# Two attentions with 32-wide heads: the three score products of a head become one product of depth 96 on copies made by DMA

## What is computed

```python
Q = split_heads(Xn @ Wq + bq)
K = split_heads(Xn @ Wk + bk)
V = split_heads(Xn @ Wv + bv)
scores = jnp.einsum('bhqd,bhkd->bhqk', Q, K) / jnp.sqrt(jnp.float32(D_HEAD))
causal = jnp.tril(jnp.ones((n_ctx, n_ctx), dtype=bool))
scores = jnp.where(causal, scores, jnp.float32(-jnp.inf))
A = jax.nn.softmax(scores, axis=-1)
AV = jnp.einsum('bhqk,bhkd->bhqd', A, V)
AV = AV.swapaxes(-2, -3).reshape(X.shape[:-1] + (D_MODEL,))
return AV @ Wo + bo
```

## Time and profile before

| | us |
|---|---|
| median of 3 runs | 3378.17 (3377.19 to 3378.65) |
| span of the profiled execution | 3376.4 |
| a0, from its first weight load to the next stage's loads | 8.2 to 383.1 |
| a1, likewise | 785.6 to about 1235 |
| PE busy in the whole span | 2992.2 (89%) |

### The profile page before, as it was taken

One profiled execution on the slowest core, in us unless ns is written; L12 is line 12 of the kernel. 1 busy time (PEld: TensorE's weight loads), 2 busy tenths in 40 slices (PEclk: granted clock), 3 DMA queues, 4 the chain that ended last, 5 costly groups with the idle time before them and its releaser, 6 DMA issues. The chain is left out here.

```text
span 3376.4 us, 46857 instructions
## 1 busy us (share of the span) xinstructions
PE 2992.2 (89%) x16388; PEld 2260.9 (67%) x16388; DVE 1996.1 (59%) x5348; ACT 1551.2 (46%) x3598; POOL 1019.2 (30%) x1143
## 2 busy tenths in 40 slices
PE   6999799997999977978788767998689999989999
PEld 4777678885666645446566646775467777768887
DVE  5666587775555554233747767664678777742121
ACT  5777566664666652133222244444455555531000
POOL 3655333222444530000156640000133233322222
PEclk9999899998999987988899988999799999999999
DMA  2000301101000021203100020003100000020000
GB/s 87 2 2 1 113 32 32 32 32 63 1 2 1 2 67 64 100 7 117 66 4 4 2 101 1 1 1 119 34 1 1 1 1 1 1 103 13 13 13 13
DMA packets 65872, 105.51 MB, mean 31 GB/s; under 512 B 9315, under 2 KB 29795, under 8 KB 65509
## 3 DMA queue, kind: packets, MB, share of 16 engines
q1 hardware_dynamic: 65222, 102.41, 8.7%
q0 software_dynamic: 416, 0.10, 0.0%
HBM read 89.75 MB, written 12.85 MB: 30 GB/s over the span
## 5 line engine op out<-in xcount | busy, mean ns | idle before, releaser
L714 POOL TENSOR_SCALAR a_P<-a_P,a_rec 128x512 f32<-128x512 f32 (+3 forms) x256 | 301.5, 1190 | 350.9 <-DVE a_rec L872 350.9
L402 ACT ACTIVATE tree_value<-tree_bit,table_lut,tree_step 128x256 f32<-128x256 uint8 x496 | 275.3, 595 | 140.8 <-DVE tree_value L416 73.0
L416 DVE COPY_PREDICATED tree_value<-tree_bit,tree_value 128x256 f32<-128x256 uint8 x434 | 235.0, 547 | 133.3 <-ACT tree_value L402 104.9
L787 ACT ACTIVATE a_P<-a_P,a_low 128x384 f32<-128x384 f32 (+3 forms) x512 | 281.7, 558 | 25.0 <-DVE a_low L866 24.9
L101 PE MATMUL bank<-f_xT_hi,f_w_hi 128*128 128x512 f32 (+1 forms) x704 | 276.6, 393 | 14.0 <-DVE f_w_lo L1214 14.0
L102 PE MATMUL bank<-f_xT_hi,f_w_lo 128*128 128x512 f32 (+1 forms) x704 | 276.1, 392 | 0.0
L103 PE MATMUL bank<-f_xT_lo,f_w_hi 128*128 128x512 f32 (+1 forms) x704 | 275.7, 392 | 0.0
L1136 POOL CAST f_h_hi<-f_sg 128x512 fp32r<-128x512 f32 (+1 forms) x88 | 84.5, 961 | 587.6 <-DVE f_sg L1236 297.8
L866 DVE CUSTOM_DVE_ANT_0 a_P<-bank,a_causal 128x384 f32<-128x384 f32 (+3 forms) x512 | 222.9, 482 | 63.1 <-PE bank L949 62.6
L794 ACT ACTIVATE a_PT<-bank 128x512 f32<-128x512 f32 x320 | 174.2, 594 | 83.3 <-PE bank L960 82.6
L1236 DVE TENSOR_TENSOR f_sg<-bank,f_sg 128x512 f32<-128x512 f32 (+1 forms) x44 | 30.4, 691 | 269.4 <-PE bank L103 269.4
(11 more groups left out here) (464 smaller groups left out, 7922.7 us busy)
## 6 DMA issues: line engine op xcount, KB each, us to landing
f_w_raw<-in_f_w SPq DMA_DIRECT2D x11, 768.0 KB, 12.8
f_w_raw<-table_w SPq DMA_DIRECT2D x11, 768.0 KB, 11.2
tree_idx<-in_f_idx SPq DMA_DIRECT2D x62, 128.0 KB, 2.1
table_w<-tree_value SPq DMA_DIRECT2D x62, 128.0 KB, 1.7
x_res<-in_x SPq DMA_DIRECT2D x4, 1024.0 KB, 10.8
m_piece<-in_m_wq SPq DMA_DIRECT2D x2, 2048.0 KB, 12.1
m_piece<-in_m_wo SPq DMA_DIRECT2D x2, 2048.0 KB, 8.5
m_piece<-in_m_w_gate SPq DMA_DIRECT2D x2, 2048.0 KB, 10.4
```

The source lines that it names most:

```text
L402: act.activation(prog.tree_value[(h + to) % 4][:, :], prog.tree_bit[h % 2][0][:, :], ACT.Identity, bias=prog.table_lut[:, 2 * k:2 * k + 1] ...
L416: dve.copy_predicated(prog.tree_value[(h + keep) % 4][:, :], prog.tree_bit[h % 2][bit][:, :], prog.tree_value[(h + other) % 4][:, :]).then ...
L714: last = pool.tensor_scalar(Pr[j][:, g, col:col + n], Pr[j][:, g, col:col + n], rec[:, j, i, g:g + 1], None, ALU.mult)
L787: last = act.activation(Pr[j][:, k, col:col + n], Pr[j][:, k, col:col + n], ACT.Exp, bias=low[:, j, i, k:k + 1], scale=-1.0, accum_out=tot ...
```

## The change

Queries and keys are no longer used where ACT and DVE write them. `Q` and `K` shrink to one chunk, a landing place. From there SP copies, SBUF to SBUF, each head's 32 partitions three times into partitions 0 to 95 of a stacked tile: `QS` as hi, lo, hi (two turns), `KS` as hi, hi, lo (two turns in a0, one in a1). That is 12 DMAs of 64 KB for each Q and 12 for each K, where a1 has 16 of either and a0 16 and 4. One matmul 96 deep for each head and part of a chunk then gives the sum of the three products.

New waits: SP waits for the low part, and before writing a turn again for the last scores that read it (for K two waits, one for each pair of heads); ACT waits, before it writes Q or K, until the copies of the one before have landed; PE waits for the copies of Q once and for those of K at each pair of a unit's first chunk. In `ORDER`, VT and Q(0, 1) of a0 and two V of a1 stand ahead of the first scores instead of among them; in a0 T and K of the next row come earlier; DVE's statistics and POOL's roots of a0 follow.

```diff
-    Q, _ = prog.pair(name + "_Q", [P, DC, T])
-    turns = 2 if KC == 1 else 1
-    K = [prog.pair(f"{name}_K{i}", [P, KC, T])[0] for i in range(turns)]
+    Q, _ = prog.pair(name + "_Q", [P, T])
+    K, _ = prog.pair(name + "_K", [P, T])
+    K_TURNS = 2 if KC == 1 else 1
+    QS = [prog.sb(f"{name}_QS{i}", [P, G, T], F32R) for i in range(2)]
+    KS = [prog.sb(f"{name}_KS{i}", [P, G, T], F32R) for i in range(K_TURNS)]
+    DEPTH = 3 * HD
+    Q_COPIES, K_COPIES = (0, 1, 0), (0, 0, 1)
...
-                     [[[("Q", b, 3)], []], [[("Y", b - 1, 2)], [("T", n, 0)]], [[("Y", b - 1, 3)], [("T", n, 1)]]],
-                     [[[("T", n, 2)], [("T", n, 3)]], [[("Q", n, 0)], []], [[("K", n, 0)], []]],
+                     [[[("Q", b, 3)], [("T", n, 0)]], [[("Y", b - 1, 2)], [("T", n, 1)]], [[("Y", b - 1, 3)], [("T", n, 2)]]],
+                     [[[("T", n, 3)], [("K", n, 0)]], [[("Q", n, 0)], []], [[], []]],
...
-        beside = [[(("VT", 0, 0), 6)], [(("V", 0, 0), 7)], [(("Q", 0, 1), 4)]]
+        ORDER += [(("VT", 0, 0), 6), (("Q", 0, 1), 7)]
+        beside = [[(("V", 0, 0), 4)], [], []]
...
+                if kind == "Q":
+                    m = unit(at, k)
+                    sp.wait_ge(*read((kind, at, k)))
+                    if m >= 2:
+                        sp.wait_ge(*full(("S", 3 * (m - 2) + 2, G - 1)))
+                    for g in range(G):
+                        for i, half in enumerate(Q_COPIES):
+                            sp.dma_start(QS[m % 2][HD * i:HD * (i + 1), g, :].bitcast(F32), Q[half][HD * g:HD * (g + 1), :].bitcast(F32)).then_inc(q_in[m % 2].sem, 16)
...
+                        if i_ >= K_TURNS:
+                            sp.wait_ge(*full(("S", k_last_chunk(i_ - K_TURNS), some[1])))
...
+                    if kind == "Q" and unit(at, k):
+                        act.wait_ge(*q_stacked(unit(at, k) - 1))
...
+                    if j == 0:
+                        if k == 0:
+                            pe.wait_ge(*q_stacked(m))
+                        pe.wait_ge(*k_stacked(i_, k))
+                    for g in (2 * k, 2 * k + 1):
                         pe.wait_ge(*vacant(("S", at, g)))
...
+                        for i, (col, qt) in enumerate(PARTS[j]):
+                            n = (qt + 1) * P
+                            last = pe.matmul(ps[J.bank(("S", at, g))][:, col:col + n], QS[m % 2][0:DEPTH, g, qt * P:(qt + 1) * P],
+                                             KS[i_ % K_TURNS][0:DEPTH, g, 0:n], start=i == 0, stop=True, skip_group_check=True)
+                        last.then_inc(J.fills(("S", at, g)), 1)
```

More of the change, by code:

```diff
@@ L649, in attention32, with unit, q_stacked, k_number @@
     NQK = DC + KC
-    def unit(at):
-        return at[0] * DC + at[1]
+    q_in = [prog.count(f"q_in{i}") for i in range(2)]
+    k_in = [[prog.count(f"k_in{i}_{k}") for k in (0, 1)] for i in range(K_TURNS)]
+    Q_BYTES, K_BYTES = 16 * len(Q_COPIES) * G, 16 * len(K_COPIES) * G // 2
+    def unit(b, c):
+        return b * DC + c
+    def q_stacked(m):
+        return q_in[m % 2](0, Q_BYTES * (m // 2 + 1))
+    def k_number(b, c):
+        return b if KC == 1 else unit(b, c)
+    def k_stacked(i, k):
+        return k_in[i % K_TURNS][k](0, K_BYTES * (i // K_TURNS + 1))
+    def k_last_chunk(i):
+        return 3 * (DC * i + DC - 1) + 2 if KC == 1 else 3 * i + 2
     def used(i):
@@ L674, in _ @@
                 sp.dma_start(bo[:, :], ins[f"{name}_bo"].partition_broadcast(P)).then_inc(w_in[3].sem, 16)
+            for kind, at, k in ORDER:
+                if kind == "Q":
[6 more added lines that the diff above has]
+                            sp.dma_start(QS[m % 2][HD * i:HD * (i + 1), g, :].bitcast(F32), Q[half][HD * g:HD * (g + 1), :].bitcast(F32)).then_inc(q_in[m % 2].sem, 16)
+                elif kind == "K":
+                    i_ = k_number(at, k)
+                    sp.wait_ge(*read((kind, at, k)))
+                    for pair_ in (0, 1):
+                        some = (2 * pair_, 2 * pair_ + 1)
+                        if i_ >= K_TURNS:
+                            sp.wait_ge(*full(("S", k_last_chunk(i_ - K_TURNS), some[1])))
+                        for g in some:
+                            for i, half in enumerate(K_COPIES):
+                                sp.dma_start(KS[i_ % K_TURNS][HD * i:HD * (i + 1), g, :].bitcast(F32), K[half][HD * g:HD * (g + 1), :].bitcast(F32))\
+                                  .then_inc(k_in[i_ % K_TURNS][pair_].sem, 16)
         @block.gpsimd
@@ L774, in _ @@
                     act.wait_ge(*full(key))
-                    to = (Q if kind == "Q" else K[at % turns])[0][:, k, :]
+                    if kind == "Q" and unit(at, k):
+                        act.wait_ge(*q_stacked(unit(at, k) - 1))
+                    if kind == "K" and k_number(at, k):
+                        for pair_ in (0, 1):
+                            act.wait_ge(*k_stacked(k_number(at, k) - 1, pair_))
+                    to = (Q if kind == "Q" else K)[0][:, :]
                     if biased:
@@ L842, in _ @@
                 elif kind in ("Q", "K"):
-                    pair = Q if kind == "Q" else K[at % turns]
+                    pair = Q if kind == "Q" else K
                     dve.wait_ge(*c_qk(0, QK_NO[key]))
@@ L936, in _ @@
                     (b, c), j = UNITS[at // 3], at % 3
[L937 to L941, removed]
-                        pe.wait_ge(*vacant(("S", at, g)))
[L943 to L952, removed]
+                    m, i_ = unit(b, c), k_number(b, c)
+                    if j == 0:
[3 more added lines that the diff above has]
+                    for g in (2 * k, 2 * k + 1):
+                        pe.wait_ge(*vacant(("S", at, g)))
+                        for i, (col, qt) in enumerate(PARTS[j]):
[3 more added lines that the diff above has]
+                        last.then_inc(J.fills(("S", at, g)), 1)
                 elif kind == "PT":
@@ L1013, in attention32 @@
     c_ot_hi.advance(NU if split_y else 0)
+    for i in range(2):
+        q_in[i].advance(Q_BYTES * NU // 2)
+    for turn in k_in:
+        for c in turn:
+            c.advance(K_BYTES * (NB if KC == 1 else NU) // K_TURNS)
 def first_rows(prog, sp, b):
```

15 lines of the change are left out of this document (8 added, 7 removed).

## The result

The changed kernel took **3406.76 us** (median; 3402.86 to 3409.98) against 3378.41 for the kernel before on the same chip: ratio 1.0081, interval 1.0066 to 1.0095. It is slower by about 28 us where 27 us of gain were forecast; the time lies outside the range given.

A forecast was written before the change was run, and what follows sets the result against it. PE was taken to bound both attentions (busy 640 of 680 us); 39.5 - 3.5 - 5 - 4 = 27 us of gain gave span 3349.4, time 3351 us, own range 3338 to 3364, 8 in 10 range 3336 to 3376.

The forecast's parts named there:

- gain that PE keeps: Scores in both attentions: cheaper products save PE 39.5 us, of which 4 us are given back to the scaling chain.
- a0: moved pieces and later copies: a0, unit 2, chunk the key projection leaves: PE idles 7 us over three rows, 2 back, so 5 us; Q copies free.
- a1: later copies: K copies in a1: hidden except at unit 2 to unit 3, where the second pair comes late; 3.5 us together.
- both heads: Start of each attention: no change, as transposes run during the wait for copies; -2 to +4 us together.
- The prices of the new products: Four heads' scores per chunk cost PE 0.92 us (512 keys), 1.16 (384 and 128), 0.48 (256), split or not.
- Serial issue: Rival 3, SP's queue: slower copy issues, from 0.86 us each, eat the gain in a1; 3462 us at 1.37; chance 0.09.
- the second rival: a0: the scaling chain's 0.31 us margin eats all 12.9 us there; 14 us gain remains, 3364 us; chance 0.12.
- the first rival: PE's scores: the loss beside the pace stays and new pairs pay half; 12.5 us gain, 3366 us; chance 0.14.
- The fourth: PE's scores: no gain, the new form pays all the excess too, costs of 12.5 us remain; 3391 us; chance 0.05.
- the signs listed as right: Score matmuls 0.23 us apart, pairs under 0.5, issues 0.5 apart, copy waits only at a1's unit 3, 2 us idle in a0.
- Those listed as wrong: a1 scores ending waits for `a_KS` in most units, pairs of 0.68 us, or waits for POOL grown in all of a0.

The follow-up runs named there:

- bare products: Changed kernel with a0's old order and only the copies that first fill each stacked buffer, scores not the reference's: 3382.72 us, ratio 1.0001.
- the best version: Changed kernel, a0's old order, old products for the first unit of each a0 row and of a1, second units' projections early: 3366.14 us, ratio 0.9962.

## Why the prediction was wrong

The forecast had a span of 3349.4 us, the profiled execution has 3407.5. With the run of bare products as the price of the products, the 58 us between them divide by the forecast's own terms (that run's profiled execution was a short one, so the gain and the copies both come out high):

| us | forecast | measured |
|---|---|---|
| gain that PE keeps (39.5 less 4) | -35.5 | -21.4 |
| a0: moved pieces and later copies | +5 | +26.8 |
| a1: later copies | +3.5 | +7.0 |
| both heads | 0 | +15.3 |
| the rest | 0 | +3.3 |

- **The moved pieces were the step that failed most.** The forecast priced them at 5 us, by POOL's scaling chain at the chunk that the key projection leaves. That idle time came in all three rows, 1.8 us each (1.08, 0.31 and 0.43 up to 216.44), most of it at the masks, but it was the small part. For the chunk that the projection enters the forecast gave 2 us back. It did not look at what the projection itself waits for there: 4.7, 4.7 and 2.8 us for T's result, which stands behind a scaling on POOL. The statistics were not priced at all. Alone the moves cost a0 35.5 us. In the changed kernel undoing them gives 13.8, because the copies are then late; with the later copies left out too, 26.8 (345.1 to 318.2).
- **The heads** were taken as no change; the first scores came 8.7 and 6.6 us late. In a0 that was forecast (39.9 for the first pair, 42.7 for the second; with 0.63 us an issue they came at 41.1 and 44.8), but nothing was to follow from it. The argument that transposes came at 51.3 anyway missed what PE does ahead of them: the scores of the third chunk, which wait for the masks of the second, which DVE makes behind the scaling of the first. That chain moved with the first scores, and the moved statistics stand in it too: the transposes came at 57.86, and with the statistics put back at 55.23. The head of a1 is not taken apart: with its key copies on ACT's queue its first score came 1.9 us sooner and 4.7 late still.
- **The copies in the body**: 3.5 us were forecast, for K in a1; leaving out all later copies gave 6.6 to 7.0 there. The windows of a1 were right: beside the head, waits above 2 us for `a_KS` come only at unit 3, in three rows. Only the price of an issue was off: 11 issues at 0.63 and a landing of 2.1 make 9.0 us against the window of 6.7, 2.3 late, and 2.1 to 2.9 us were waited there. For a0 the forecast called copies of Q hidden and gave K no price; with the old order the rows' first scores wait, and the later copies cost 13.0 us in all. So the move had a purpose, and cost more than it saved.
- **The prices of the new products were nearly right**: a single pair of 512 keys 0.46 us as forecast where it stands behind a projection, 0.56 to 0.57 where it stands behind PV or T (84.39 to 84.96); 384 and 128 together 1.19 for four heads (forecast 1.16). Four heads of 512 unsplit, which stand behind PV as well, cost 1.03 (forecast 0.92) against 0.91 before, a little worse, the one place where the Trainium skill's rule that row strips run side by side (TensorE: Matmul & The Clock Gate, "Part 3: Packing small matmuls") agreed with the trace, and the change does lose there.
- **What PE keeps of the gain was wrong.** 39.5 us were priced and a tenth given back. Counted from start to next start, scores in a0 occupied PE for 74.9 us before, where the forecast's own prices sum to 53.8: of the 21.1 between them 14.8 are idle time, most of it for masks, and a0's idle time did not shrink with bare products (33.1 us against 25.7, the head's waits for copies in it). Bare products gained 15.6 to 21.4 us over both attentions, with first units that still waited for copies; the best version gained 14.4 in the bodies.
- **The rivals.** Serial issue, on the slower side, was to eat the gain in a1 from 0.86 us on; at 0.63 it didn't decide there. Issue did cost, at the heads, which no rival named. That a0 gives nearly nothing, the second rival's outcome, came near with bare products (4.8 of 12.9 us), though PE waited for masks there and not for the scaling; of the first rival's loss beside the pace, 0.1 us of 0.22 showed, behind PV and T. The fourth, no cheaper products at all, did not come. Of the signs listed as right, the step of 0.23 us, the idle time at unit 2 and the copies late at unit 3 came, lone pairs under 0.5 us only behind projections, issues 0.5 us apart not at all. Those listed as wrong did not come in this form: the waits grew at DVE's masks and at `a_xT_lo`.

Open stays how much of the lower clock belongs to each wait; only the moves alone separate it, 13.6 us. No cause is shown for the 3.3 us of the rest.

## What to carry to other kernels

Price a moved piece at the place where it arrives: what the instruction ahead of it must still pass through, what stands on those queues first, and whose queue its companions lengthen. Count DMAs, not bytes, where many small ones go through one queue, and look first at the head of a stage, where nothing covers them. Where a cheaper operation needs preparation, keep the old form for the few units whose preparation stands on the path, and prepare the next ones early: the old form alone left the time at 3378.9 us, both together gave 3366.1.

## What the runs showed of the hardware

- A copy from SBUF to SBUF costs its issuing queue 0.63 to 0.64 us on SP, whether it moves 16, 64 or 128 KB, and the same on ACT at 64 KB; it lands after 1.8, 2.0 and 2.4 us (medians). With twelve of them on its queue ACT stood idle for 8.47 us ahead of its next eviction.
- After 4.68 us without work PE ran at the lower clock level for 3.2 us; after 0.99 us ahead of the first projection behind T it did not. In a changed order the same 3024 matmuls of a0 were busy 13.6 us longer, at a mean clock of 0.91 in place of 0.95, beside 21.9 us more idle time.
